# A reordered instruction schedule in a macaron block (expert layer, windowed attention, expert layer): the ones rows, the head order and the table of places

## The reference

```
x = x + 0.5 * ffn(layernorm(x))     # 8 experts, top 2, capacity 1.25 * 8192 / 8 = 1280 tokens
x = x + attention(layernorm(x))     # 16 heads of 16, |i - j| <= 128, and token 0 attends and is attended by all
x = x + 0.5 * ffn(layernorm(x))
```

## Time and profile before

| | us |
|---|---|
| median of 3 runs | 843.41 (840.58 to 843.43) |
| the profiled execution | 843.41 |
| its span | 841.6 |
| TensorE matmul busy | 809.3 (96%) |
| VectorE, ScalarE, GpSimd busy | 730.9, 610.3, 524.5 |

### The profile page before, as it was taken

How to read it: one execution, slowest core, us unless ns; L and a number is a source line. 1 busy time by engine, 2 the same in 40 slices (tenths; PEclk the granted TensorE clock), 3 DMA queues, 4 the chain that set the end, 5 groups by cost and what they waited for, 6 DMA issues and landing times.

```text
span 841.6 us, 50562 instructions
## 1 busy us (share of the span) xinstructions
PE 809.3 (96%) x21494; PEld 618.2 (73%) x21495; DVE 730.9 (87%) x2787; ACT 610.3 (73%) x1387; POOL 524.5 (62%) x888
## 2 busy tenths in 40 slices
PE   7899999999999999999999999999999999999997
PEld 7655767778788787677778777777778778776675
DVE  6899899998977899998987799998987789999864
ACT  3325778897877667888777766888787766788970
POOL 2355756896554556888554466789554465766772
PEclk9999999999999999999999999999999999999999
DMA  8342225332213235442222244533221323424003
GB/s 240 90 98 68 83 76 135 112 112 69 82 59 117 91 116 151 123 130 69 89 94 66 82 143 129 148 98 100 68 79 62 114 95 103 134 78 128 7 28 107
DMA packets 93210, 83.55 MB, mean 99 GB/s; under 512 B 17584, under 2 KB 92208, under 8 KB 92976
## 3 DMA queue, kind: packets, MB, share of 16 engines
q1 hardware_dynamic: 91376, 78.91, 30.7%
q10 hardware_dynamic: 1600, 1.31, 0.8%
HBM read 20.66 MB, written 8.39 MB: 35 GB/s over the span
## 4 chain that ended last, share of the span: by engine, by line
PE 76%; DVE 9%; ACT 6%; issue 3%; POOL 3%; SPq 1%; ACTq 1%; DMA 1%; DVEq 0%; POOLq 0%
PE bank L1128 15%; PE bank L1076 12%; PE bank L1110 12%; PE bank L965 11%; PE bank L947 7%; PE bank L980 6%; DVE bank L1535 5%; PE bank L1150 3%; ACT probs L1259 3%; PE bank L933 2%; PE bank L885 2%; PE bank L900 1%; ACT pieces L1209 1%; PE bank L1020 1%; DVE row_max L1535 1%
## 5 line engine op out<-in xcount | busy, mean ns | idle before, releaser
L1259 ACT ACTIVATE probs<-bank 128x384 f32<-128x384 f32 (+1 forms) x1024 | 457.1, 479 | 144.1 <-PE bank L1110 127.6
L1535 DVE CUSTOM_DVE_ANT_0 bank<-bank,con 128x288 f32<-128x288 f32 x1024 | 493.4, 514 | 58.4 <-PE bank L1076 52.4
L1076 PE MATMUL bank<-k_stack,q_stack 96*32 96x288 bf16 x4096 | 334.1, 288 | 7.1 <-DVE row_max L1535 4.2
L1110 PE MATMUL bank<-q_stack,k_stack 99*32 99x288 bf16 (+3 forms) x4096 | 326.3, 284 | 5.8 <-ACT probs L1259 2.1
L1128 PE MATMUL bank<-probs,v_sb 128*32 128x128 f32 x5888 | 314.5, 272 | 4.6 <-issue 1.7
L1339 POOL TENSOR_SCALAR_AFFINE_SELECT probs<-probs 128x512 f32<-128x512 f32 x240 | 154.7, 644 | 135.4 <-ACT probs L1259 134.4
L1128 PEld LDWEIGHTS bank<-probs,v_sb 128*32 128x32 f32 x5888 | 200.8, 110 | 34.3 <-issue 5.8
L1076 PEld LDWEIGHTS bank<-k_stack,q_stack 96*32 96x32 bf16 x4096 | 134.8, 95 | 68.1 <-DVE row_max L1535 25.2
L1110 PEld LDWEIGHTS bank<-q_stack,k_stack 99*32 99x32 bf16 x4096 | 131.1, 95 | 57.1 <-ACT probs L1259 34.4
L1344 POOL TENSOR_SCALAR_AFFINE_SELECT probs<-probs 128x512 f32<-128x512 f32 x240 | 152.8, 637 | 21.1 <-ACT probs L1259 21.1
L965 PE MATMUL bank<-xnT,wqk_sb 128*32 128x256 f32 x2048 | 160.3, 379 | 0.1
(11 more groups left out here) (124 smaller groups left out, 738.3 us busy)
## 6 DMA issues: line engine op xcount, KB each, us to landing
q_stack<-pieces SPq DMA_DIRECT2D x384, 64.0 KB
k_stack<-pieces SPq DMA_DIRECT2D x364, 64.0 KB
x_ring<-in_x SPq DMA_DIRECT2D x28, 512.0 KB, 5.3
out_x<-x_ring SPq DMA_DIRECT2D x15, 512.0 KB, 3.7
attn<-in_x SPq DMA_DIRECT2D x4, 512.0 KB, 6.2
wback_sb<-in_wback SPq DMA_DIRECT2D x8, 256.0 KB, 5.5
k_stack<-pieces ACTq DMA_DIRECT2D x20, 64.0 KB
q_stack<-neg_max SPq DMA_DIRECT2D x48, 16.0 KB, 2.4
```

The lines of the kernel that those rows point to most:

```text
L1076: last = pe.matmul(a_ring[i % len(a_ring)][SP * s:SP * (s + 1), 0:WIN], q_stack[g % 2][0:KROWS, h, q:q + SP], k_stack[g % 2][0:KROWS, h, q ...
L1110: last = pe.matmul(score_bank(i)[SP * s:SP * (s + 1), start:final], k_stack[g % 2][0:SROWS, h, WINDOW + P * j + SP * s:WINDOW + P * j + SP ...
L1259: act.activation(probs[:, j % 4, h, c0:c1], score_bank(i)[:, c0:c1], ACT.Exp, scale=LOGIT_SCALE).then_inc(S["exp_ready"], 1)
L1535: dve.tensor_tensor_reduce(out=a_ring[i % len(a_ring)][:, 0:WIN], in0=a_ring[i % len(a_ring)][:, 0:WIN], in1=mask, scale=1.0, scalar=con[: ...
```

## The change

- WARM is 36 instead of 31 matmuls.
- ORDER_HEADS is a VectorE copy, placed behind chunk 0's MOMENTS, instead of a ScalarE one.
- K_ONES is a ScalarE activation (Copy of a broadcast 3 x 2304), at quarters 45, 53, ..., 101, instead of a GpSimd memset behind PIECE3.
- In `deviations`, the multiplication for `neg_mean` is issued between `var_eps` and the power for `rstd`, no longer after it.
- QK waits for both halves of the chunk's XT_IN before its first part.
- Nearly all tables of places move by a few quarters.

```diff
-        WARM = 31
+        WARM = 36
...
-        QK_AT = (-43, -28, -10, 5, 23, 41, 53, 68, 83, 101, 118, 134, 149, 165, 178, 202)
-        QK_APART = (2, 3, 2, 2, 2, 2, 1, 3, 1, 1, 1, 1, 1, 1, 2, 2)
-        ONES_FROM = 2
-        STACK_LAG = 20
-        VALUES_AT_OPENING = (36, 47, 57, 63, 66, 80, 89, 94)
-        VALUES_APART_OPENING = (1, 1, 1, 0, 2, 1, 1, 0)
-        FIRST_AT_OPENING = (10, 22, 32, 44, 50, 60, 103, 106, 137)
-        EARLY_AT = (-79, -64, -49, -31)
-        EARLY = {'LOAD': -18, 'MOMENTS': (0, 3, 6, 7), 'RSTD': 10, 'NORM': (11, 13, 14, 18), 'XT': 19}
+        QK_AT = (-43, -28, -7, 5, 23, 41, 52, 68, 83, 102, 118, 134, 149, 165, 178, 202)
+        QK_APART = (2, 3, 3, 2, 2, 2, 1, 3, 1, 1, 1, 1, 1, 1, 2, 2)
+        STACK_LAG = 23
+        VALUES_AT_OPENING = (36, 47, 56, 61, 71, 80, 88, 94)
+        VALUES_APART_OPENING = (1, 1, 1, 2, 2, 1, 1, 0)
+        FIRST_AT_OPENING = (17, 22, 32, 44, 54, 55, 102, 112, 133)
+        EARLY_AT = (-79, -64, -49, -32)
+        EARLY = {'LOAD': -19, 'MOMENTS': (1, 3, 6, 7), 'RSTD': 9, 'NORM': (12, 12, 14, 18), 'XT': 19}
...
-        EARLY_AT_OPENING = (-68, -49, -39, -30)
-        XT_AT_OPENING = (-55, -31, -18, 9)
-        QK_AT_OPENING = (-44, -26, 2, 14, 25, 39, 52, 69, 85, 98, 124, 131, 153, 162, 182, 201)
-        OPENING = {'ORDER_HEADS': -79, 'WBACK': -53, 'FOLD': 175, 'FILL': 21, 'QK_APART': 1, 'STACK': 5, 'STACKS': 12}
-        LATE_AT = (95, 115, 131, 146)
+        EARLY_AT_OPENING = (-62, -52, -44, -35)
+        XT_AT_OPENING = (-40, -31, -24, 6)
+        QK_AT_OPENING = (-38, -30, 1, 14, 25, 39, 52, 68, 84, 101, 123, 133, 153, 161, 178, 198)
+        OPENING = {'ORDER_HEADS': -55, 'WBACK': -52, 'FOLD': 174, 'K_ONES': 45, 'FILL': 20, 'QK_APART': 1, 'STACK': 4, 'STACKS': 12}
+        LATE_AT = (99, 115, 131, 146)
...
-        STORE_AT = (381, 396, 400, 416, 618, 641, 659, 679, 878, 923, 916, 937)
+        STORE_AT = (381, 397, 405, 420, 625, 637, 667, 679, 886, 910, 918, 933)
...
-                    if first and ONES_FROM <= 4 * n + c < ONES_FROM + 2 * HG:
-                        end(done + 2, "K_ONES", n, c)
...
+                for i in range(2 * HG):
+                    end(OPENING["K_ONES"] + 8 * i, "K_ONES", *divmod(i, HG))
...
-                pool.wait_ge(S["eps_added"], i + 1)
-                pool.tensor_tensor(rstd[:, i % 2, :], var_eps[:, :], neg_half[:, :], ALU.pow)\
-                    .then_inc(S["rstd_ready"], 1)
                 if phase == "EARLY":
...
                     pool.tensor_scalar(neg_mean[:, b % 2, tiles], mean_var[:, i % 2, :, 0], -1.0, None,
                                        ALU.mult).then_inc(S["move_ready"], 1)
+                pool.wait_ge(S["eps_added"], i + 1)
+                pool.tensor_tensor(rstd[:, i % 2, :], var_eps[:, :], neg_half[:, :], ALU.pow)\
+                    .then_inc(S["rstd_ready"], 1)
...
+                                pe.wait_ge(*emptied("XT", early_index[g // NG, c], 1))
                                 claim(pe, "QK", g, c)
-                            if k == 0:
-                                pe.wait_ge(*emptied("XT", early_index[g // NG, c], half))
...
-                        elif kind == "ORDER_HEADS":
-                            act.wait_ge(S["wqk_in"], 16)
-                            act.activation(
-                                wqk_sb[:, :, :, :].rearrange("p g k (x d h) -> p (g k x) d h", x=2, h=HG),
-                                wqk_raw.rearrange("p (x h d) -> p x d h", h=HG, d=HD), ACT.Copy).then_inc(S["wqk_ready"], 1)
...
+                        elif kind == "K_ONES":
+                            stack, h = n
+                            act.activation(k_stack[stack][KROWS:SROWS, h, :].rearrange("p (a b) -> p a b", b=P),
+                                           ones[KROWS:SROWS, :].unsqueeze(1)
+                                           .to_broadcast([SROWS - KROWS, (T + 2 * WINDOW) // P, P]),
+                                           ACT.Copy).then_inc(S["k_ones"], 1)
...
-                        elif kind == "K_ONES":
-                            g, c = n
-                            i = 4 * g + c
-                            stack, h = divmod(i - ONES_FROM, HG)
-                            pool.wait_ge(S["piece3_ready"], i + 1)
-                            pool.memset(k_stack[stack][KROWS:SROWS, h, :], 1.0).then_inc(S["k_ones"], 1)
-                            pool.wait_ge(S["k_ones"], i - ONES_FROM + 1)
...
+                        elif kind == "ORDER_HEADS":
+                            dve.wait_ge(S["wqk_in"], 16)
+                            dve.tensor_copy(
+                                wqk_sb[:, :, :, :].rearrange("p g k (x d h) -> p (g k x) d h", x=2, h=HG),
+                                wqk_raw.rearrange("p (x h d) -> p x d h", h=HG, d=HD)).then_inc(S["wqk_ready"], 1)
```

More of the change, by code:

```diff
@@ L393, in build @@
-        OPENING = {'ORDER_HEADS': -79, 'WBACK': -53, 'FOLD': 175, 'FILL': 21, 'QK_APART': 1, 'STACK': 5, 'STACKS': 12}
-        LATE_AT = (95, 115, 131, 146)
+        QK_AT = (-43, -28, -7, 5, 23, 41, 52, 68, 83, 102, 118, 134, 149, 165, 178, 202)
+        QK_APART = (2, 3, 3, 2, 2, 2, 1, 3, 1, 1, 1, 1, 1, 1, 2, 2)
+        STACK_LAG = 23
+        VALUES_AT = (33, 48, 57, 61, 70, 80, 88, 92)
+        VALUES_APART = (2, 2, 0, 2, 2, 2, 1, 2)
+        VALUES_AT_OPENING = (36, 47, 56, 61, 71, 80, 88, 94)
@@ new lines, in build @@
+        VALUES_APART_OPENING = (1, 1, 1, 2, 2, 1, 1, 0)
+        LOGITS_LAG = -2
+        FIRST_AT = (-17, -8, 15, 32, 50, 60, 96, 112, 135)
+        FIRST_AT_OPENING = (17, 22, 32, 44, 54, 55, 102, 112, 133)
+        FIRST_APART = (1, 2, 1, 2, 1, 4, 3, 1, 4)
+        EARLY_AT = (-79, -64, -49, -32)
+        EARLY = {'LOAD': -19, 'MOMENTS': (1, 3, 6, 7), 'RSTD': 9, 'NORM': (12, 12, 14, 18), 'XT': 19}
+        NORM_ENGINES = ("gpsimd", "scalar")
+        EARLY_AT_OPENING = (-62, -52, -44, -35)
+        XT_AT_OPENING = (-40, -31, -24, 6)
@@ L395, in build @@
+        QK_AT_OPENING = (-38, -30, 1, 14, 25, 39, 52, 68, 84, 101, 123, 133, 153, 161, 178, 198)
+        OPENING = {'ORDER_HEADS': -55, 'WBACK': -52, 'FOLD': 174, 'K_ONES': 45, 'FILL': 20, 'QK_APART': 1, 'STACK': 4, 'STACKS': 12}
+        LATE_AT = (99, 115, 131, 146)
         LATE_AT_END = (52, 68, 85, 102)
-        LATE = {'LOAD': -13, 'TURN_ATTN': 2, 'PROJECT': ((7, 8, 10, 10), (12, 12, 15, 15)), 'BASE': -13, 'MOMENTS': (12, 18, 18, 19), 'RSTD': 21, 'STORE': 25}
+        LATE = {'LOAD': -10, 'TURN_ATTN': 2, 'PROJECT': ((7, 8, 10, 10), (12, 12, 14, 15)), 'BASE': -2, 'MOMENTS': (12, 18, 18, 19), 'RSTD': 23, 'STORE': 16}
@@ L397, in build @@
         LATE_END = {'TURN_ATTN': 0, 'PROJECT': ((6, 6, 8, 9), (12, 15, 15, 15)), 'BASE': -2, 'MOMENTS': (12, 16, 16, 23), 'RSTD': 35, 'STORE': 24}
-        LOAD_AT = (150, 164, 188, 214, 351, 346, 373, 388, 417, 427, 445, 459, 572, 610, 627, 635, 646, 678, 685, 717, 863, 869, 891, 907, 988, 1000, 1006, 1129)
-        STORE_AT = (381, 396, 400, 416, 618, 641, 659, 679, 878, 923, 916, 937)
-        WBACK_AT = (214, 471, 723)
+        LOAD_AT = (157, 172, 194, 203, 355, 355, 371, 388, 419, 434, 447, 466, 589, 623, 624, 651, 663, 675, 689, 722, 848, 880, 896, 913, 1010, 1016, 1018, 1100)
@@ L401, in build @@
+        STORE_AT = (381, 397, 405, 420, 625, 637, 667, 679, 886, 910, 918, 933)
+        WBACK_AT = (218, 468, 740)
         COUNT_AT = 16
         FLAG_AT = (6, 6)
-        OUT_AT = (-1, -1, 4, 3, -1, -1, -1, 1, -1, 8, 1, 0, 0, 1, 3, 0)
+        OUT_AT = (0, 0, 0, 3, -1, -1, -1, 1, -1, 8, 1, 0, 0, 1, 3, 0)
         OUT = {'TURN': 0, 'ADD': 0, 'RECIP': 1, 'MULT': 2}
@@ L739, in deviations @@
                                        ALU.mult).then_inc(S["move_ready"], 1)
+                pool.wait_ge(S["eps_added"], i + 1)
+                pool.tensor_tensor(rstd[:, i % 2, :], var_eps[:, :], neg_half[:, :], ALU.pow)\
+                    .then_inc(S["rstd_ready"], 1)
+                if phase == "EARLY":
                     pool.wait_ge(S["rstd_ready"], i + 1)
```

4 lines of the change are left out of this document (removed).

## The result

The changed kernel takes **850.90 us** in the median (848.76 to 853.37, 7 runs), the kernel before on the same chip 843.41 (840.58 to 847.84, 7 runs). The ratio is **1.0088, 95% interval [1.0065, 1.011]**: slower by 7.4 us (5.5 to 9.3), under 1% but clear of the scatter. The forecast was 842.9 with a range of 837.5 to 847.5; both missed. The profiled execution took 850.0, 6.6 more than the profiled one of before, with a span of 848.2.

What follows compares the result with a forecast made beforehand. VectorE was taken to bound 28 to 73 us and TensorE the rest after. Sum: 843.41 - 2.4 (opening) + 3.1 (copies) - 0.35 (memsets) - 0.9 (boundaries) = 842.9 us, range 837.5 to 847.5.

Steps and rivals of the forecast that it cites:

- The opening, -2.4: Start to the VectorE-bound stage: removing TensorE's 3.48 us idle gap lets 2.4 us of gain through, bounds 0.5 and 3.3.
- ScalarE's DMA issue: Opening: five DMA issues of chunk 0, 3.42 us on ScalarE, would be what is late next, not TensorE.
- no TensorE gap over 2 us before 28: Trace sign for the opening: TensorE has no gap over 2 us before 28 us.
- K_ONES, +3.1 - 0.35: Copies on ScalarE cost 3.1 us at 73 to 92 us; dropping GpSimd's memsets gives 0.35 back.
- the slow rival: ScalarE, quarters 80 to 105: copies run at the strided rate, 4.2 us each, total 849.2 us; chance 0.08.
- three of 1: Trace sign: behind the last three K_ONES copies TensorE waits for probs, about 1 us each.
- at worst 0.3 each: Quarters 45 to 77, before the first exponential: five K_ONES copies cost nothing, at worst 0.3 us each.
- Batch boundaries, -0.9: Batches 1 to 3: NORM at (12, 12) gets transposes their xn earlier, gaining 0.3 us a boundary; bounds -3 and +3.
- the third rival: Cuts 1.2 us late stall PV at each of 12 normalised chunks by about 0.5 us, total 849.8; chance 0.07.
- STACK_LAG, LOAD_AT, STORE_AT and LATE_AT change only what passes what: Batches 1 to 3: these tables only reorder work on SP and GpSimd; STACK stays 16 quarters ahead of its first reader.
- The sign that the prediction itself had named: The prediction would be wrong if boundary stretches of 200 us differ by over 1 us.

Runs made afterwards that it cites:

- e4: The kernel before with the changed opening and batch 0's places, neg_mean order and QK wait, K_ONES still on GpSimd: median 848.3 us, slower by 5.5 us.
- e1: The changed kernel with K_ONES back on GpSimd as memsets behind PIECE3, all else changed: 849.07 us.
- e3: The changed kernel with the places of batches 1 to 3 as before, except FIRST_APART: 850.27 us, ratio 1.0086.
- e2: The kernel before with only K_ONES moved to ScalarE at quarters 45 to 101: 847.71 us, slower by 5.5 us.
- e8: e7 with K_ONES on ScalarE, four copies ahead of the first chunk and four at quarters 45 to 69: ratio 1.0031 to the kernel before.
- e10: The kernel before with only the normalisation plan EARLY changed for batches 1 to 3: slower by 2.7 us.
- e9: The kernel before with the new places of batches 1 to 3 but the old normalisation plan (EARLY, EARLY_AT): ratio 1.0043, slower by 3.6 us.
- e6: The kernel before with only the new places of batches 1 to 3, FIRST_APART as before: ratio 1.0071, slower by 6.0 us.
- e7: The kernel before with the changed opening plus 10 filler matmuls before pass A, batch 0's places from quarter 0 as before: 843.9 us, ratio 1.0014.
- e5: e4 with 10 filler matmuls of ones between chunk 2's transposes and the first pass A: 849.7 us, ratio 1.0072 to the kernel before.

## Why the prediction was wrong

**The opening, -2.4: right where it was read, -2.5 at the first strip.** QK of chunk 1 was forecast for 20 and came at 19.20, PIECE1 of chunk 3 for 37.0 and came at 36.59 (39.38 before), the first pass A for 26.0 and came at 26.12, the clock at 20 to 23 us was 1.00. What stood late next was named wrong, though: not ScalarE's DMA issue, which for chunk 1 ended at 27.3 instead of 30.0, but the landing of the stacks. The first pass A waited 2.09 us for them (so "no TensorE gap over 2 us before 28" failed by a hair; 2.15 and a clock drop in e4), QK of chunk 2 stood behind it, and PIECE1 of chunk 2 waited for that QK until 29.26. That the total came out is in part luck. The wait also makes the gain fragile: where the clock fell behind it (e1, e3, e4), the gain was gone by strip 4. An issue is still not small for ScalarE, 2.63 us for four. The Trainium skill's page DMA: Bandwidth & Descriptors (Issuing engines are not separate DMA queues) calls the time to start a DMA usually small beside the DMA itself; whether it would have been the better guide to this stage no run here shows.

**K_ONES, +3.1 - 0.35: right in size, wrong in place.** Measured 2.3 to 2.4 net by profiles and 1.7 by the ratios, in company: 3.4 for the copies, and -1.1, not -0.35, for the memset that no longer delays a cut. A copy took 2.12 us against 2.1; the view is not strided, the slow rival falls, and the 2.1 us that the prediction took from rows holds. But of the late copies one wait of 1.31 and one of 0.29 came, not three of 1, and of the early ones, "at worst 0.3 each", a single one cost 1.0 us (e2, e8): it holds up a copy to v_sb that frees a PSUM bank (1.05 us at 66.78 in e2). Alone, in e2, the same edit cost 5.5, with a second long wait at 96.34 and 1.6 us of low clock behind it.

**Batch boundaries, -0.9: this step failed, and in its sign.** It priced XT's wait for the second xn (0.44 us, gone) and took for granted that PV, 12 quarters behind, absorbs later cuts. It doesn't: PV waits 0.8 us at each of three boundaries, and net of the waits that went, each boundary costs 0.3 to 0.5 instead of giving 0.3: +1.3 in all, and about 1.7 more where the clock falls behind one (e10). By the ratios the plan alone costs 2.7 (e10). That was the third rival, held at 0.07; its place and its size (0.5) were right, its count was not, 3 places and not 12 chunks. "STACK_LAG, LOAD_AT, STORE_AT and LATE_AT change only what passes what" was half of an argument: passing is what costs, and the tables other than the normalisation plan cost 3.6 without it (e9), the largest part of the batches' 6.0 (e6), and by which waits stays open. The sign that the prediction itself had named came too: over 256 strips, about 200 us, the changed kernel loses 2.4 and then 2.2 us more (strips 256 to 512, 512 to 768), though e7's profile moves as much.

**Batch 0's quarters: the step that was missing.** The sum had no term for QK_AT_OPENING, VALUES_AT_OPENING and FIRST_AT_OPENING from quarter 0 on, although they begin in the most loaded stage, VectorE at 42.97 of 45 us. Measured +2.4 to +2.8 in the profiles at strip 128, +4.9 by the ratios (e5 against e7, FIRST_APART of the later batches with it).

The account of the two profiles is then: -2.5 to strip 0; +1.0 to strip 63, with a clock drop at 39.2; +4.7 from 63 to 128, half copies and half batch 0's places; -0.9 to strip 256; +4.3 to the end, where 1.3 is shown at the three boundaries and the rest is the batches' other places and the scatter of one profile, which can't be told apart. It sums to 6.6. By the ratios the parts don't add up: e2, e6 and e4 alone cost 5.5, 6.0 and 5.5, all together 7.4. Why they don't wasn't settled. One reading fits, but no run tests it: any departure from an order tuned by hand may bring waits and with them low clock, and a second departure then costs less than the first.
